# Second layer normalisation: two 512-column instructions on GpSimd, or four two-step instructions of 128 columns on VectorE

## The reference

```python
h = jnp.maximum(_layernorm(x, axis=-1), 0.0)
x = x + _L0_gnn_ref(h, adj, L0_gnn_weight, L0_gnn_w_ih, L0_gnn_w_hh, L0_gnn_b_ih, L0_gnn_b_hh)
h = jnp.maximum(_layernorm(x, axis=-1), 0.0)
x = x + _L1_gnn_ref(h, adj, L1_gnn_W, L1_gnn_a)
return x
```

## Time and profile before

| | |
|---|---|
| median of three runs | 474.96 us (474.70 to 475.09) |
| the profiled execution | 474.28 us, of which 472.5 us from the first to the last instruction |
| TensorE busy | 456.6 us, 97% |
| DVE busy | 426.0 us, 90% |
| ACT busy | 355.2 us, 75% |
| POOL busy | 142.2 us, 30% |
| mean granted TensorE clock | 0.995 of full speed |

### The profile page before, as it was taken

The page is one execution under the profiler, slowest core; times in us unless marked ns, Lnnn a source line. Parts: engine busy times, 40 slices in busy tenths (PEclk is TensorE's granted clock), DMA queues, the critical chain, the costliest instruction groups (busy, mean ns, idle before and its releaser), DMA issues.

```text
span 472.5 us, 8260 instructions
## 1 busy us (share of the span) xinstructions
PE 456.6 (97%) x2644; PEld 386.0 (82%) x2644; DVE 426.0 (90%) x1085; ACT 355.2 (75%) x640; POOL 142.2 (30%) x169
## 2 busy tenths in 40 slices
PE   8799999999999999999999999999999999998986
PEld 7577787788888888888888888888888888887875
DVE  4878998999999999999999999999999999988863
ACT  3457667778978797887879787897879788677484
POOL 3222444232423224232422323242322423133300
PEclk9989999999999999999999999999999999999999
DMA  8400020300203030210203020020302000000001
GB/s 332 175 1 0 2 111 1 112 3 27 109 22 112 24 111 12 45 80 24 111 24 112 24 76 37 28 107 24 111 24 113 9 15 2 22 2 22 24 2 45
DMA packets 7243, 26.43 MB, mean 56 GB/s; under 512 B 800, under 2 KB 800, under 8 KB 5152
## 3 DMA queue, kind: packets, MB, share of 16 engines
q1 hardware_dynamic: 7200, 25.90, 15.1%
HBM read 21.70 MB, written 4.19 MB: 55 GB/s over the span
## 4 chain that ended last, share of the span: by engine, by line
PE 85%; DVE 7%; ACT 5%; issue 2%; POOL 1%; DMA 1%; DVEq 0%; SPq 0%
PE X L1187 18%; PE G L1303 11%; PE G L1292 5%; PE R L1171 5%; PE R L1173 4%; PE Z L1173 4%; PE Z L1171 4%; PE R L1172 4%; PE Z L1172 4%; PE X L1237 3%; PE G L1270 3%; PE IN L1173 2%; PE IN L1171 2%; PE HN L1171 2%; PE IN L1172 2%; PE HN L1173 2%
## 5 line engine op out<-in xcount | busy, mean ns | idle before, releaser
L1187 PE MATMUL X<-A_ring,nat_hi 128*128 128x512 f32 x192 | 79.0, 411 | 1.0 <-DVE nat_lo L747 1.0
L1187 PE MATMUL X<-A_ring,nat_lo 128*128 128x512 f32 x192 | 76.0, 396 | 0.0
L1303 PE MATMUL G<-hp,probT 128*128 128x128 f32 x512 | 65.3, 275 | 0.7 <-DVE out_sb L864 0.7
L1303 PEld LDWEIGHTS G<-hp,probT 128*128 128x128 f32 x512 | 62.2, 192 | 2.1 <-issue 0.9
L852 DVE SCALAR_TENSOR_TENSOR prob<-e 128x512 f32<-128x512 f32 x64 | 48.2, 753 | 9.3 <-ACT e L444 8.0
L382 ACT CAST agg_hi<-X 128x512 fp32r<-128x512 f32 x48 | 28.1, 586 | 34.5 <-PE X L1187 34.4
L262 POOL TENSOR_TENSOR hT_lo<-hT,hT_hi 128x512 fp32r<-128x512 f32 x19 | 24.5, 1290 | 92.0 <-ACT hT_hi L370 72.2
L402 ACT ACTIVATE tr<-R,bias 128x512 f32<-128x512 f32 x48 | 33.4, 695 | 24.6 <-PE R L1173 24.6
L443 ACT ACTIVATE e<-g,nb 128x512 f32<-128x512 f32 x64 | 46.3, 724 | 6.7 <-DVE nb L845 6.7
L444 ACT ACTIVATE e<-g,nb 128x512 f32<-128x512 f32 x64 | 45.7, 714 | 0.0
L1187 PEld LDWEIGHTS X<-A_ring,nat_hi 128*128 128x128 f32 x192 | 36.5, 190 | 11.1 <-DVE nat_lo L747 3.0
(11 more groups left out here) (127 smaller groups left out, 1210.8 us busy)
## 6 DMA issues: line engine op xcount, KB each, us to landing
adj_raw<-in_adj SPq DMA_DIRECT2D x16, 1024.0 KB, 5.1
x_ring<-in_x SPq DMA_DIRECT2D x16, 256.0 KB, 2.7
out_x<-out_sb SPq DMA_DIRECT2D x16, 256.0 KB, 2.0
inner_in<-in_inner SPq DMA_DIRECT2D x1, 384.0 KB, 6.0
outer_in<-in_outer SPq DMA_DIRECT2D x1, 325.0 KB, 5.5
```

Source lines behind the costliest of these rows:

```text
L1187: mm = pe.matmul(X[:], part[s][:, c], A_ring[:, (k - s) % RING, c], start=(c == 0 and part is nat_hi), stop=(c == C - 1 and part is nat_lo))
L1303: mm = pe.matmul(G2[:, c * D:(c + 1) * D], probT[:, c % 2, j], hp[:, (k + 1) % 2, j, 0:D], start=(j == 0), stop=(j == C - 1))
```

## The change

POOL keeps only `scale2`. `centre2`, POOL's `normed2` and the buffer `x2c` go. DVE gets a `normed2` that subtracts the mean and multiplies by the reciprocal root in one instruction for each chunk, both scalars read per partition. It is called once in each iteration from 3 to 18, at a place written out by hand.

```diff
-            def centre2(i, k):
-
-                if on(i, GA):
-                    pool.wait_ge(mv2_done, (i - (GA - 1)) * C)
-                    pool.tensor_tensor(x2c[:], x2[:, k % 2], mv2[:, :, 0:1].broadcast_to([P, C, D]),
-                                       ALU.subtract).then_inc(x2c_done, 1)
-
             def scale2(i, k):
...
-            def normed2(i, k):
-
-                if on(i, GA):
-                    pool.wait_ge(x2c_done, i - (GA - 1))
-                    pool.wait_ge(rstd2_done, i - (GA - 1))
-                    pool.tensor_tensor(h2n[:], x2c[:], rstd2[:].rearrange("p (c o) -> p c o", o=1).broadcast_to([P, C, D]),
-                                       ALU.mult).then_inc(h2n_done, 1)
-
             def full(i):
-                centre2(i - 1, (i - 1) % RING)
                 scale2(i - 1, (i - 1) % RING)
-                normed2(i - 1, (i - 1) % RING)
                 norm_scale(i, i % RING)
...
+            def normed2(i, k):
+
+                if on(i, GA):
+                    dve.wait_ge(rstd2_done, i - (GA - 1))
+                    for c in range(C):
+                        nd = dve.tensor_scalar(h2n[:, c], x2[:, k % 2, c], mv2[:, c, 0:1], rstd2[:, c:c + 1], ALU.subtract, ALU.mult)
+                    nd.then_inc(h2n_done, 1)
+
```

The calls of centre2 and normed2 in POOL's written-out iterations go likewise. DVE's calls stand so (one line of context on either side):

```diff
                 state_low(i, i % RING, 0)
+                normed2(i, i % RING)
                 reset(i, i % RING, 1)
...
             natural_low(3, 3, 1)
+            normed2(3, 3)
             adjacency(3, 3)
...
             probabilities(18, 2, 0)
+            normed2(18, 2)
             probabilities(18, 2, 1)
```

More of the change, by code:

```diff
@@ L126, in graph_block @@
         rstd2 = sb("rstd2", [P, C])
-        x2c = sb("x2c", [P, C, D])
         h2n = sb("h2n", [P, C, D])
@@ L178, in graph_block @@
         g_turned, x2_done, st2_done, mv2_done = (sem(n) for n in ("g_turned", "x2_done", "st2_done", "mv2_done"))
-        eps2_done, rstd2_done, x2c_done, h2n_done = (sem(n) for n in ("eps2_done", "rstd2_done", "x2c_done", "h2n_done"))
+        eps2_done, rstd2_done, h2n_done = (sem(n) for n in ("eps2_done", "rstd2_done", "h2n_done"))
         h2_turned, h2T_done, fj_mm, hp_mm = (sem(n) for n in ("h2_turned", "h2T_done", "fj_mm", "hp_mm"))
@@ L307, in _ @@
             natural_low0(3, 3)
-            centre2(3, 3)
-            normed2(3, 3)
             norm_scale(4, 0)
@@ L316, in _ @@
                 full(i)
-            centre2(15, 3)
             scale2(15, 3)
-            normed2(15, 3)
             state_low(15, 3, 1)
-            centre2(16, 0)
             scale2(16, 0)
-            normed2(16, 0)
             state_low(16, 0, 2)
-            centre2(17, 1)
             scale2(17, 1)
-            normed2(17, 1)
             scale2(18, 2)
-            centre2(18, 2)
-            normed2(18, 2)
         @block.scalar
@@ L1027, in _ @@
             state_low(4, 0, 0)
+            normed2(4, 0)
             reset(4, 0, 1)
@@ L1069, in _ @@
             reset(15, 3, 1)
+            normed2(15, 3)
             new_state(15, 3, 2)
@@ L1097, in _ @@
             probabilities(16, 0, 2)
+            normed2(16, 0)
             keep(16, 0, 2)
@@ L1118, in _ @@
             probabilities(17, 1, 2)
+            normed2(17, 1)
             reset(17, 1, 2)
```

## The result

The change makes the kernel slower: 484.84 us (median of four executions, 484.68 to 489.21) against 475.02 us before on the same chip (474.70 to 475.14), a ratio of 1.023 with a 95% interval of 1.0172 to 1.0287: slower beyond doubt, though not surely by 2%. The profiled execution took 484.88 us, 10.6 more than the profiled one before, with a span of 483.0 us and a mean granted TensorE clock of 0.993.

The account below looks back on a forecast made before the run. TensorE was taken to set the 27.00 us period, DVE having about 1.1 us to spare. Loop 2.6, iteration 3 3.4, iteration 18 2.6 and clock 1.5 made 10.1 us on 474.28: 484.4, as median 485.0; range 479.5 to 488.5.

Parts of the forecast that it names:

- The price of an instruction: One new 128-column DVE instruction with two per-partition scalars: 0.346 us, 0.266 from start to start, 1.06 for four.
- The relief of POOL: In the loop, DVE's two-input instruction is no longer slowed by POOL's centring: 0.30 us given back.
- The loop: Iterations 4 to 14: DVE 0.70 us late against a margin of 0.46, so 0.24 lost in each, 2.6 us in all.
- Iteration 3: DVE waits 2.3 us for the reciprocal root, POOL's natural_low0 holds its first new instruction, TensorE loses 3.4 us.
- Iteration 18: Last stage: the new call stands behind probabilities waiting for ACT's exponentials, so the transposes and ACT's relu come 2.6 us late.
- Iterations 15 to 17: Iteration 15 loses nothing; in 16 and 17 instructions that POOL delayed win back the four's cost, within 0.2 us.
- The clock: TensorE's clock falls to half rate after the long waits in iterations 3 and 18: 1.5 us, counted once.
- no loop wait: Rival: only the two ends and the clock cost, 7.1 us, giving 482, or 480.5 without a clock fall; chance 0.30.
- the slow rate: Rival: DVE instructions with two scalars run at one element per cycle, 13.4 us lost, giving 488.4; chance 0.10.
- short waits: Rival: POOL doesn't come between in iteration 3, clock stays up, no loop wait: 4.6 us, giving 479.6; chance 0.10.
- the other side: Rival: POOL gives up its hold on DVE and nothing is paid, at most 0.30 us gained, giving 474.7; chance 0.02.
- nothing changes: Rival: both ends are absorbed by waits that were not seen, 475.0 us; chance 0.03.

Follow-up runs that it names:

- one_scalar: The changed kernel with the number 0.0 in place of the mean as first scalar, so one per-partition scalar is read instead of two: 483.79 us.
- order_loop: The changed kernel with layer 2's new state moved behind the fourth probabilities in iterations 4 to 14: 482.14 us.
- hold_pool3: The changed kernel with iteration 18's call moved as in early18 and, in iteration 3, POOL's natural_low0 held until DVE has made layer 1's agg_lo: 480.35 us.
- late3: The changed kernel with iteration 3's DVE normed2 moved from ahead of adjacency(3) to behind x_stats(4): 480.83 us.
- idle28: The changed kernel with 28 instead of 14 identity products on TensorE ahead of the last transposes in iteration 18: 484.31 us.
- after_again: The changed kernel itself, unedited, run again on another chip beside idle28: 488.05 us, six executions from 483.97 to 489.24.
- early18: The changed kernel with iteration 18's DVE normed2 moved from behind the first probabilities to ahead of them, behind the offsets: 481.61 us.
- ends_moved: The changed kernel with the moves of late3 and early18 together: 477.93 us.
- all_moved: The changed kernel with the moves of late3, early18 and order_loop, and iteration 16's normed2 behind its fourth probabilities: 474.73 us, ratio 1.0009.

## Why the prediction was right

**The price of an instruction** was taken as 0.346 us, from rows that each lacked one part of it; it is 0.341. From start to start 0.266 was forecast for each, and 1.06 for four; 1.03 came. The second scalar costs about what the first does: 0.220 without, 0.285 with one, 0.341 with two. The estimate from the Trainium skill, "VectorE: DVE Perf Modes", section on the TRN2 errata, was 0.127 us for one and 0.51 for four. The measurement differs, with 0.258 and 1.03, and it decides; the page's warning that small tiles pay the fixed part each time goes the way of the rows.

**The relief of POOL** was put at 0.30 for the probability; it is 0.32, 0.67 against 0.99.

**The loop** was the step with the least margin: 0.24 us in each of eleven iterations, left over from a lateness of 0.70 and a margin of 0.46. Measured were 27.25 against 27.00, and 2.80 in all against 2.6. Two experiments take the step apart from either side: less work (one_scalar), and all the work with one instruction moved behind the wait (order_loop), and each brings 27.00 back. By the rows its terms are these: npre ends 8.42 us behind `turn_input` of its iteration (213.98 against 205.56) and before 7.78 (208.95 against 201.17), so DVE was 0.64 late and not 0.70. IN starts 0.15 behind that end, as much as was taken off the margin for the release and the weight load together; that was a choice, and no run splits it. 0.64 - 0.46 = 0.18 is IN's late start, and the 0.08 by which its matmul is longer comes on top. One term was too large by 0.06 and 0.08 was missing, so that 0.24 came so near is in part luck.

**Iteration 3**: a DVE wait of 2.3 us (2.25), a first instruction held by natural_low0 (1.31), rv 3.8 late (3.72), 3.4 lost (3.39). The alternative, that POOL doesn't come between and 2.4 are lost, is hold_pool3, with 0.97 less; the mechanism is shown from both sides.

**Iteration 18**: 2.6 forecast, 2.60 measured on the way from the probability to the relu. TensorE's idle time of 3.6 was 3.29, since TensorE came to it 6.56 us later than before (455.97 against 449.41) and DVE's probability only 6.23.

**Iterations 15 to 17** were put at nothing within 0.2, and it was 0.04 at the probability of 18.

**The clock** was right in size for the first profiled execution, and wrong in place. I counted 1.5 us once and put it rather behind iteration 3, "since TensorE is full behind the first and its order has waits behind the second". In the profiled execution it fell behind the second and not behind the first; 1.67 us went there, of which late3 and idle28 show 1.47 to be the clock's. The rest of 0.2 is there without a fall too: from the relu to the terms late3 takes 2.72 us against 2.53 before. It goes with TensorE's order, by the rows: the ten matmuls of `idle(18, 0, 5)` used to be through before the relu was (451.18 against 451.69), and now `project` stands behind them. That it is they was only read, not tried. Nor is "once" right in general: the profiled execution with one fall took 484.88 us, the one with two 489.24, above the range's 488.5, and on the second chip five of six lay above 487. That the first measurement's median came within 0.2 us of the forecast is in part luck: three of its four executions had the mean clock of 0.993 of the profiled one, with its single fall.

**The sum** of 10.1 us against 10.5 of span is thus right by its terms in that execution, with 0.2 too little in the loop and 0.2 at the end. Of the rivals, *no loop wait* and *the slow rate* failed at the price of an instruction, *short waits* at the 2.25 and 3.29 us of waiting, *the other side* and *nothing changes* at all three places.

## What to carry to other kernels

When work moves to another engine, its total time says little: here 16 calls cost 10 us, by late results at three places and by the clock that fell at long waits, and another order in one queue brought it back without taking out one instruction. Price each call where it stands: what the engine does between there and its next real wait, and who waits for that. In a pipeline with a loop, look at the first and the last iteration by themselves, since a step that fits into the loop can stand there in front of everybody.

## What the runs showed of the hardware

- A lower clock at a TensorE wait isn't a fixed price. The same kernel, with the same waits of 3.15 to 3.29 us, saw it fall at one place (484.88 us) or at two (489.24); late3's tail, with a wait of 3.29, saw none. At the end, from the transposes to the terms, a fall cost 1.47 us with 3.4 us at 0.50 (the changed kernel) and 2.61 with 6.7 (after_again); order_loop's cost 1.64. In iteration 3 it cost 2.5 (after_again).
- What decides it between executions stays open, but the rows show a pattern: the three profiled executions with a wait of 2.95 to 3.19 us and a fall in iteration 3 (one_scalar, after_again, idle28) are ones in which the clock at the start had fallen before 22 us; in the three with such a wait and no fall there (the changed kernel's first, early18, order_loop) it was at 1.00 until 22 us. No run tests whether one follows from the other.
- Whether long waits also cost in spread isn't settled. The changed kernel spread over 4.5 and 5.3 us (four and six executions) and ends_moved over 1.0 (six), but order_loop, with waits of 3.18 and 3.29, over only 0.6 (four), all_moved, without them, over 2.7 (twelve), and the kernel before over 3.6 (23, 472.8 to 476.39).
- A DVE `tensor_scalar` with one tensor input is held by a two-input instruction of POOL that started just ahead of it, 0.97 us here (hold_pool3). A DVE instruction of two inputs took 1.27 us in the same position.
- POOL's power of 128x4 elements and the step ahead of it read 1.33 and 1.09 in the earlier trace rows, beside A_ring and rv on DVE; with DVE standing they took 1.04 and 0.23. That DVE held them is read from the rows, not tried.
